# Attention with decay and a mixture of experts: the chain of states moved in front of the scan of decays on VectorE

## What is computed

```python
def step(carry, inp):                       # per batch and head (16 heads of 64)
    S, z = carry
    qt, kt, vt, at = inp                    # q, k = elu(.) + 1; a = sigmoid(x @ Wa + ba + 2)
    S = at[..., None, None] * S + kt[..., :, None] * vt[..., None, :]
    z = at[..., None] * z + kt
    num = jnp.einsum('bhk,bhkv->bhv', qt, S)
    den = jnp.einsum('bhk,bhk->bh', qt, z) + eps
    return ((S, z), num / den[..., None])
```

## Time and profile before

| What | us |
|---|---|
| Median of 3 runs | 3340.37 |
| Lowest and highest run | 3338.11, 3342.51 |
| The profiled execution's own time | 3338.53 |
| Its span, from the first to the last instruction | 3336.8 |
| TensorE busy in the span | 3224.1 (97%) |
| VectorE busy | 2442.7 (73%) |
| ScalarE busy | 1815.1 (54%) |
| GpSimd busy | 1434.8 (43%) |

### The profile page before, as it was taken

How to read it: one execution, slowest core, us unless ns; L and a number is a source line. 1 busy time by engine, 2 the same in 40 slices (tenths; PEclk the granted TensorE clock), 3 DMA queues, 4 the chain that set the end, 5 groups by cost and what they waited for, 6 DMA issues and landing times. The chain is left out here.

```text
span 3336.8 us, 128741 instructions
## 1 busy us (share of the span) xinstructions
PE 3224.1 (97%) x50858; PEld 2737.6 (82%) x50858; DVE 2442.7 (73%) x6617; ACT 1815.1 (54%) x4492; POOL 1434.8 (43%) x1117
## 2 busy tenths in 40 slices
PE   7999999999999999999999999999977999999999
PEld 6888888888888888888888888888865888878887
DVE  6777777777777777777777777777746787878786
ACT  5666666666666666666666666666632322222221
POOL 4444445545544454455455444444431222222222
PEclk9999999999999999999999999999997999999999
DMA  4222222222232222222222322222212111111110
GB/s 151 79 74 77 81 79 79 79 73 76 84 90 79 77 78 78 79 79 79 73 76 81 93 79 76 77 79 79 73 49 77 52 39 39 52 39 39 52 39 26
DMA packets 158608, 238.66 MB, mean 72 GB/s; under 512 B 30216, under 2 KB 82488, under 8 KB 157752
## 3 DMA queue, kind: packets, MB, share of 16 engines
q1 hardware_dynamic: 158008, 230.33, 21.9%
HBM read 194.58 MB, written 35.67 MB: 69 GB/s over the span
## 5 line engine op out<-in xcount | busy, mean ns | idle before, releaser
L447 POOL TENSOR_TENSOR qs_sb<-lam_bc,qk_sb 128x512 f32<-128x512 f32 x256 | 532.7, 2081 | 1069.0 <-DVE qk_sb L946 966.3
L554 ACT ACTIVATE kd_sb<-bank_scores,decay 128x64 f32<-128x64 f32 x2048 | 447.9, 330 | 285.4 <-PE bank_scores L822 276.1
L929 DVE SCALAR_TENSOR_TENSOR s_mid<-s_mid,lam_bc,bank_dense 128x65 f32<-128x65 f32 x1536 | 433.4, 282 | 54.8
L455 POOL TENSOR_TENSOR oT_lo<-oT,oT_hi 128x512 fp32r<-128x512 f32 x256 | 328.4, 1283 | 77.7 <-ACT oT_hi L531 77.7
L513 ACT ACTIVATE qk_sb<-bank 128x512 f32<-128x512 f32 x512 | 317.3, 620 | 52.5 <-PE bank L596 36.8
L1141 POOL TENSOR_TENSOR acc<-acc,gb 128x512 f32<-128x512 f32 x64 | 83.1, 1299 | 581.3 <-DVE acc L1313 558.2
L515 ACT ACTIVATE qk_sb<-qk_sb 128x512 f32<-128x512 f32 x512 | 323.3, 631 | 16.3
L981 DVE TENSOR_TENSOR p_sb<-bank_scores,decay 128x512 f32<-128x512 f32 x256 | 176.6, 690 | 202.2 <-ACT kd_sb L554 199.5
L952 DVE TENSOR_TENSOR_SCAN decay<-a_bc,eye 128x512 f32<-128x512 f32 x256 | 310.8, 1214 | 2.7 <-DMA a_bc<-rows_dram 2.4
L594 PE MATMUL bank<-wv_hi,h_hi 128*128 128x256 f32 x1024 | 306.8, 300 | 4.8 <-DVE qk_sb L944 4.1
L1313 DVE SCALAR_TENSOR_TENSOR acc<-bank,comb,acc 128x256 f32<-128x256 f32 x512 | 229.7, 475 | 105.6 <-ACT acc L1181 96.3
(11 more groups left out here) (198 smaller groups left out, 8561.4 us busy)
## 6 DMA issues: line engine op xcount, KB each, us to landing
a_bc<-rows_dram SPq DMA_DIRECT2D x512, 128.0 KB, 3.1
lam_bc<-rows_dram SPq DMA_DIRECT2D x512, 128.0 KB
x_in<-in_L_attn_x_dram SPq DMA_DIRECT2D x32, 512.0 KB, 6.0
x_res<-in_L_attn_x_dram SPq DMA_DIRECT2D x32, 512.0 KB, 4.1
x_dram<-x_res SPq DMA_DIRECT2D x32, 512.0 KB, 2.9
x<-x_dram SPq DMA_DIRECT2D x32, 512.0 KB, 3.3
out_dram<-x SPq DMA_DIRECT2D x32, 512.0 KB, 3.0
ew_raw<-in_L_ffn_expert_W_dram SPq DMA_DIRECT2D x8, 256.0 KB, 5.6
```

What stands on the lines that cost most here:

```text
L447: pool.tensor_tensor(qs_sb[:, na, :], lam_bc[na][:, :], q_sb, ALU.mult).then_inc(qs_ready, 1)
L455: pool.tensor_tensor(oT_lo[:, u, :], oT32[:, :], oT_hi[:, u, :].bitcast(F32), ALU.subtract).then_inc(oT_lo_ready, 1)
L554: ins = act.activation(kd_sb[:, t, hd * DH:(hd + 1) * DH], KTR[:, hd, t * CK:(t + 1) * CK], ACT.Copy, scale=decay[:, hd, t, CK - 1:CK])
L929: dve.scalar_tensor_tensor(dst, src, lam_bc[nb][:, (ch + 1) * CK - 1:(ch + 1) * CK], U[ch], ALU.mult, ALU.add).then_inc(state_step, 1)
```

## The change

In VectorE's `step`, the call of `chain` for pair b now stands in front of the scan of decays for pair a. No instruction is added or taken away, and no tile or semaphore differs.

```diff
--- before.py
+++ after.py
@@ -945,14 +945,14 @@
                     dve.wait_ge(q_exp, a + 1)
                     dve.scalar_tensor_tensor(q_sb, Q[:, :], 1.0, q_sb, ALU.add, ALU.max).then_inc(q_ready, 1)
 
+                if exists(Tb):
+                    chain(Tb, place_b, sb_, pb, b)
                 if exists(Ta):
 
                     after(dve, p_ready, a)
                     dve.wait_ge(a_loaded[na], (Ta * (PAIRS // 2) + pa // 2 + 1) * 32)
                     dve.tensor_tensor_scan(decay[:, :, :, :].rearrange("p h t i -> p (h t i)"), a_bc[na][:, :],
                                            eye8[:, :, :].rearrange("p c i -> p (c i)"), 0.0, ALU.mult, ALU.add).then_inc(decay_ready, 1)
-                if exists(Tb):
-                    chain(Tb, place_b, sb_, pb, b)
                 if u != 7:
                     dense_out(T, s, u, 1)
                 if leads(T):
```

## The result

| | before | changed |
|---|---|---|
| Median, us | 3341.44 (4 runs) | 3411.93 (4 runs) |
| Lowest and highest | 3338.11, 3347.20 | 3410.65, 3412.73 |
| The profiled execution's own time | 3338.53 | 3412.73 |

What follows compares the result with a forecast made beforehand. TensorE, 98% busy, sets the pace. Losing 1.29 us in each of 31 groups makes 40 us, taking the profiled 3338.5 to 3378.5; the median stands 1.9 above, so 3380 us, range 3362 to 3399.

Steps and rivals of the forecast that it cites:

- the ring: Light steps 4 to 7: scan, kd_sb, relu and exp of k and q, maximum of q, scan again; 8.54 us a turn.
- The slack in front of kd_sb, 1.62 us, and its loss: Before the change kd_sb waits 1.62 us past the scan's end for the scores; the scan starting 2.40 us later exceeds that.
- The chain keeps its price of 2.40 us: On VectorE, the chain's eight dependent instructions take 2.40 us in either place.
- the scan runs 1488.21 to 1489.42: Step 5 of group 18 on VectorE: the scan's forecast times in its new place, its length kept at 1.21 us.
- in front of both: 0: GpSimd's qs_sb hangs on the maximum of q, ahead of chain and scan, so the move costs it 0.
- The lateness of kd_sb in steps 4, 5 and 6: 0.82, 1.64, 2.47 us: On ScalarE, kd_sb starts later than before by 0.82, 1.64 and 2.47 us, adding up from turn to turn.
- ScalarE has no gap from kd_sb to the exp of q: Step 5: ScalarE works without a gap from kd_sb to the exp of q, so the maximum of q starts at 1485.20.
- TensorE loses 1.00 us in step 6 and 0.29 in step 7: The v job waits for k: it starts 1.00 us late in step 6 and 0.29 us more in step 7.
- 0.38 us of margin: Step 5: k is ready at 1484.55, the v job starts at 1484.93, so TensorE still has what it needs.
- Steps 0 to 3 lose nothing: Scores come late enough, or in step 3 the next step waits for the lambda row, swallowing 0.7 us of lateness.
- the two together take the same time in either order: On VectorE, chain and scan ahead of the lambda row's scan: the edit leaves that row's times, a 15.3 us wait, unchanged.
- SyncE's queue costs nothing, the expert phase keeps its time, the clock stays: SyncE's lam_bc and a_bc loads cost 0; expert phase unchanged; rival of TensorE's clock falling, 3520 us, chance 0.03.

Runs made afterwards that it cites:

- e1: Changed kernel with only four of the chain's eight links in front of the scan and four behind: 3352.2 us, 1.0026 against the kernel before.
- e4: Changed kernel with GpSimd's oT_lo subtraction cut to 16 of 512 columns, the rest staying zero: 3377.0 us, 1.0097 against the kernel before.
- e9: Changed kernel, nothing left out, with GpSimd's oT_lo waiting for the step's scan of decays: 3377.4 us, 1.0104 against the kernel before.
- e6: Changed kernel with six of the chain's eight links in front of the scan and two behind: 3443.4 us, 1.0304 against the kernel before.

## Why the prediction was wrong

The direction and the mechanism, the ring, held, and two thirds of the loss lie in the steps that were named. One term was mis-sized, the plainest one; a second, smaller error went the other way and hid part of it.

- *The slack in front of kd_sb, 1.62 us, and its loss.* Right. kd_sb starts right behind the scan in steps 4 to 6, and in step 3 as well, and e1, which stays inside the slack, loses 9 us of 70.
- *The chain keeps its price of 2.40 us.* Right: 2.42.
- *"the scan runs 1488.21 to 1489.42", and so each scan at 1.21 us.* **This step failed.** The forecast took a duration from the place where the instruction used to stand. There it began 0.2 us ahead of GpSimd's qs_sb, and it was GpSimd that paid, with 2.13 us for work of 1.29. In its new place it mostly begins behind oT_lo and pays itself: 1.42 us on average, 1.45 and 1.35 in group 18. e4 and e9 take the overlap away in two ways, and both fall to 3377: the scans' extra length cost 34 to 36 us that the sum did not have. The forecast said of GpSimd only that its qs_sb was "in front of both: 0", and never asked what stood beside the scan afterwards.
- *The lateness of kd_sb in steps 4, 5 and 6: 0.82, 1.64, 2.47 us.* Counted from the scores of step 4, which stand 45.18 us later than before (1524.07 against the row below), it was 1.08, 1.85 and 2.69. The first scan's stretch is in all three. The turns of the ring took 8.49 and 8.55 us, as forecast (8.54), although each held a longer scan. That is luck: the forecast also said that ScalarE has no gap from kd_sb to the exp of q, and carried over a turn that has one. Before, the relu of q starts 0.71 us behind the exp of k, 0.08 us behind its end (1483.01, the rows below); in the changed kernel it starts 0.54 us behind it, which gave back as much as the scan took. Without the stretch (e4) the turns take 8.35 and 8.42 us (medians), 0.1 to 0.2 less than forecast, and step 6 loses 23 us in place of 31. So 3377 lies only 3 us from the forecast's 3380 partly by luck, since the scattered losses filled up what the ring did not take.

```profile
1478.89 1.10 PE L822 MATMUL bank_scores<-qk_sb 64*64 64x128 f32 x32
```

```profile
1482.38 0.63 ACT L515 ACTIVATE qk_sb<-qk_sb 128x512 f32<-128x512 f32 x1
1483.09 0.60 ACT L513 ACTIVATE qk_sb<-bank 128x512 f32<-128x512 f32 x1
```

- *TensorE loses 1.00 us in step 6 and 0.29 in step 7.* By the same count the v jobs of steps 5, 6 and 7 came 0.11, 1.33 and 1.73 us late in group 18: the first is one that the forecast let pass with 0.38 us of margin, and U of step 6 came 0.59 us late, where the forecast's own kd_sb, ended at 1491.21, would have made it some 0.09 late.
- *Steps 0 to 3 lose nothing.* Wrong for the same reason: behind scans of 1.47 us in steps 1 and 2 (the median over the groups) VectorE is late with p_sb and with k in step 3 (8 us in all), and the lambda row's scan stands behind a longer one (6 us), so that "the two together take the same time in either order" fails too. In e4 and e9 both losses are gone.
- *SyncE's queue costs nothing, the expert phase keeps its time, the clock stays.* Right; the granted clock was 0.991 in both.

The Trainium skill (SBUF — State Buffer, SBUF: two separate sides) describes what the rows show: a VectorE operation with two SBUF inputs and a GpSimd operation that reads SBUF contend for a shared pair of ports, which is an exclusive lock, and whichever starts first keeps the other out for its whole length. By that rule the scan (a_bc and the unit matrix, both in SBUF) would have to wait for the rest of oT_lo, and the chain, whose U lies in PSUM, would not. The trace agrees in both: the scan ends 1.08 to 1.09 us behind oT_lo's end (0.12 us less than its length alone), and the chain keeps its 2.42 us beside qs_sb. It does not agree for every instruction's whole reported length: the scan of e4 that begins with 0.52 us of xn left is not held at all. The prediction could have used the rule: oT_lo would have been seen beside the scan's new place, where the changed kernel's steps 1 to 7 add 0.14 to 0.25 us each (medians). The section of the Trainium skill that the prediction did weigh (VectorE: DVE Perf Modes, The DRAIN you can't avoid) made no difference; it adds that a next operation that is not held starts earlier, and the trace agrees: the next instruction began 0.08 us before the scan's reported end after the change as before it (1526.24 against 1526.32 in step 4).

What stays open: the 34 us of the stretch were not split between the steps by a run of their own, only by place in the trace; where the further 31 us of e6 come from in full; and why xn does not hold the scan as oT_lo does.

## What to carry to other kernels

A duration read from a trace belongs to its place: before an instruction is moved, look at what the other engines will be doing at the new time, and above all whether it used to be the one that others waited for. Where a ring of engines has slack, count the lateness per turn; the wait that shows first (VectorE's k in step 6) need not be the bound, and removing it may only move the wait to the next step. A semaphore wait on an engine with time to spare can be a gain: holding GpSimd's oT_lo back behind the scan made one kernel 109 us faster.

## What was not expected of the hardware

- The scan of 128 x 512 takes 1.21 us alone or when it begins first, and 2.09 us when it begins 0.27 us behind a GpSimd subtraction of 128 x 512; the GpSimd instruction takes 1.29 us alone and 2.13 when it begins 0.17 us behind the scan (1477.44 against 1477.27). In each case the second one ends about 1.08 to 1.09 us after the first, not its whole length after it. The profile shows the wait as a longer duration, not as idle time. A GpSimd instruction on xn (128 x 256) with 0.2 to 0.6 us left did not make the scan longer.
- Moving the scan earlier can end it no sooner and cost more: with eight links in front the kernel lost 70 us, with six 101, and with six and GpSimd held back it gained 6.
